# Graph attention in groups of four units instead of two

## The reference, cut to what matters

```python
for l in range(L):
    q = ((x @ Wq[l].T + bq[l]) * scaling).reshape(n, H, DH)
    k = (x @ Wk[l].T).reshape(n, H, DH)
    v = (x @ Wv[l].T).reshape(n, H, DH)
    scores = jnp.einsum('ehd,ehd->eh', q[tgt], k[srcidx])
    m = jax.ops.segment_max(scores, tgt, num_segments=n)
    p = jnp.exp(scores - m[tgt])
    s = jax.ops.segment_sum(p, tgt, num_segments=n)
    w = p / (s[tgt] + 1e-16)
    agg = jax.ops.segment_sum(w[:, :, None] * v[srcidx], tgt, num_segments=n)
    attn = agg.reshape(n, D) @ Wo[l].T + bo[l]
    ...
```

## Time and profile before

| | |
|---|---|
| median of 3 runs | 1277.33 us |
| all runs | 1277.33, 1277.38, 1270.37 us |
| the profiled execution | 1275.12 us |
| its span, first to last instruction | 1273.3 us |
| mean granted TensorE clock | 0.956 of 2.4 GHz |

### The profile page before, as it was taken

The page is one execution under the profiler, slowest core; times in us unless marked ns, Lnnn a source line. Parts: engine busy times, 40 slices in busy tenths (PEclk is TensorE's granted clock), DMA queues, the critical chain, the costliest instruction groups (busy, mean ns, idle before and its releaser), DMA issues.

```text
span 1273.3 us, 14957 instructions
## 1 busy us (share of the span) xinstructions
PE 1126.0 (88%) x5662; PEld 701.1 (55%) x5666; DVE 675.9 (53%) x1188; ACT 397.5 (31%) x538; POOL 201.2 (16%) x129
## 2 busy tenths in 40 slices
PE   2698999999988399999999999999989999999934
PEld 1122464447876388675566666643456666674412
DVE  7998521155556930542665556544145555663496
ACT  1001110216533211210554546411045454551103
POOL 5200000056950624200000000000000000003000
PEclk9799989989998799999999999999999999999967
DMA  5000101100020011001000001001100000100001
GB/s 190 17 0 1 34 1 33 33 0 34 1 67 0 1 33 67 34 1 66 1 1 1 1 1 68 1 21 46 33 1 1 1 1 1 34 1 19 1 0 66
DMA packets 16887, 28.98 MB, mean 23 GB/s; under 512 B 3834, under 2 KB 5050, under 8 KB 16570
## 3 DMA queue, kind: packets, MB, share of 16 engines
q1 hardware_dynamic: 14746, 26.03, 6.1%
q10 hardware_dynamic: 2080, 2.10, 0.5%
HBM read 26.02 MB, written 2.10 MB: 22 GB/s over the span
## 4 chain that ended last, share of the span: by engine, by line
PE 83%; DVE 11%; ACT 2%; issue 2%; DMA 1%; POOL 0%; DVEq 0%; SPq 0%; ACTq 0%
PE slots L1382 73%; PE slots L1449 10%; DVE PT L1209 1%; DVE KS L1199 1%; DVE st L857 1%; DVE XN L870 1%; DMA X<-in_x 1%; ACT KS L782 1%; DVE PT L921 0%; DVE SM L1263 0%; DVE X L1275 0%; DVE XT L1157 0%; DVE st L1280 0%; DVE XT L1178 0%; DVE st L847 0%
## 5 line engine op out<-in xcount | busy, mean ns | idle before, releaser
L1382 PE MATMUL slots<-XT,W 128*128 128x512 f32 x448 | 202.2, 605 | 0.0
L1382 PEld LDWEIGHTS slots<-XT,W 128*128 128x128 f32 x448 | 84.4, 193 | 105.5 <-issue 103.8
L1382 PE MATMUL slots<-PT 128*128 128x512 bf16 (+2 forms) x420 | 105.3, 381 | 31.0 <-issue 29.1
L876 DVE COPY PT<-slots 128x1024 f32<-128x1024 f32 x66 | 80.7, 1222 | 85.9 <-PE slots L1449 70.1
L1382 PE MATMUL slots<-KS,QS 64*128 64x512 f32 x768 | 108.4, 415 | 18.0 <-DVE KS L1199 9.9
L1382 PE MATMUL slots<-PT,XN 128*64 128x256 f32 x1024 | 117.6, 382 | 0.0
L601 POOL TENSOR_TENSOR QS<-QF,QS 128x512 fp32r<-128x512 f32 x16 | 20.6, 1286 | 555.1 <-PE slots L1449 359.9
L632 ACT ACTIVATE PT<-slots 128x1024 f32<-128x1024 f32 x70 | 71.6, 1023 | 106.8 <-PE slots L1449 54.3
L1382 PEld LDWEIGHTS slots<-KS,QS 64*128 64x128 f32 x768 | 73.3, 190 | 39.5 <-issue 10.0
L1382 PEld LDWEIGHTS slots<-PT,XN 128*64 128x64 f32 x1024 | 70.7, 137 | 42.9 <-issue 9.8
L1209 DVE CUSTOM_DVE_ANT_0 PT<-slots,MASK 128x1024 f32<-128x1024 f32 x64 | 75.8, 1222 | 31.7 <-PE slots L1382 31.7
(11 more groups left out here) (309 smaller groups left out, 1631.3 us busy)
## 6 DMA issues: line engine op xcount, KB each, us to landing
X<-in_x SPq DMA_DIRECT2D x1, 2048.0 KB, 8.4
W<-in_v SPq DMA_DIRECT2D x2, 1024.0 KB, 10.9
W<-in_k SPq DMA_DIRECT2D x2, 1024.0 KB, 10.1
W<-in_wout SPq DMA_DIRECT2D x2, 1024.0 KB, 5.2
W<-in_q SPq DMA_DIRECT2D x2, 1024.0 KB, 5.1
W<-in_gv SPq DMA_DIRECT2D x2, 1024.0 KB, 8.4
W<-in_gq SPq DMA_DIRECT2D x2, 1024.0 KB, 5.0
W<-in_gk SPq DMA_DIRECT2D x2, 1024.0 KB, 5.2
```

What stands on the lines that cost most here:

```text
L876: nc.vector.tensor_copy(dst, src).then_inc(dve_evacuated, 1)
L1382: return nc.tensor.matmul(o_, lhsT, rhs, start=start, stop=stop)
```

## The change

The list advances by four units at a time. Where it had two `turn`, two `score`, two `turn`, two `score`, it has four `turn` and then four `score`. The distance `LAG` = 4 between a unit's score and its transposition in the loop's counters stays. The other steps (`q`, `k`, `rsum`, `rsum_bc`, `agg`) go to the nearest places behind the four scores. No instruction is added or removed, and the code of the engines is the same.

```diff
 def attention_order():
 
     order = [("q", 0), ("q", 1), ("k", 0)]
-    for n in range(0, UNITS + LAG + 4, 2):
+    for n in range(0, UNITS + LAG + 8, 4):
         m = n - LAG
         if 0 <= m < UNITS:
-            order += [("turn", m), ("turn", m + 1)]
+            order += [("turn", m + i) for i in range(4)]
         if n < UNITS:
-            order += [("score", n), ("score", n + 1)]
-        if m >= 16 and m % 16 == 2:
+            order += [("score", n + i) for i in range(4)]
+        if m >= 16 and m % 16 == 4:
             order.append(("rsum_bc", m // 16 - 1))
-        if n % 8 == 2 and 8 <= n < UNITS - 8:
+        if n % 8 == 0 and 8 <= n < UNITS - 8:
             order.append(("q", n // 8 + 1))
-        if n % 16 == 6 and n < UNITS - 16:
+        if n % 16 == 4 and n < UNITS - 16:
             order.append(("k", n // 16 + 1))
         if m >= 16 and m % 16 == 0:
             order.append(("rsum", m // 16 - 1))
-        if m >= 4 and m % 4 == 0:
+        if 4 <= m <= UNITS:
             order.append(("agg", m // 4 - 1))
     return order
```

## The result

The changed kernel takes 1307.17 us (median of four, 1303.65 to 1309.12) against 1276.3 us before (1270.37 to 1277.38). The ratio is 1.0249, with a 95% interval from 1.0209 to 1.0288: slower, by 30.9 us between the medians. The profiled execution took 1307.08 us for a span of 1305.2, so the span grew by 31.9 us.

What follows compares the result with a forecast made beforehand. TensorE's own instruction stream and its standstills were taken to bound the kernel. Per layer 21.0 + 0.5 + 0.6 - 7.0 + 3.0 = +18.1 us, both +36.2, so 1277.3 + 36 = 1313 us, range 1298 to 1330.

Steps and rivals of the forecast that it cites:

- The stall: Before `turn` n + 3 in every group, TensorE waits 1.69 us for an exponential queued behind a copy on ScalarE.
- Merging: On TensorE, four transposed and four scored units take 6.67 against 6.96 us, 0.29 us less in each group.
- the forecast's rival: In the attention, no stall, so faster: -9.0 us a layer, 1259 us; 3% for faster by over 1%.
- Waits that go: TensorE's waits on keys, `nm` and `AG`, and at the layer's end, shrink or vanish: -7.0 us a layer.
- The wait of `project`: At the layer's end, `project` waits some 0.4 us for the copy of an `agg`, before 0.90 for unit 63's.
- Waits that come: Jobs behind four scores wait for slots on TensorE: +3 us a layer, ranging from 0 to 6.
- The first job behind four scores: It takes unit n's slot, freed at 3.04 against 2.96 us: 0.08 us each, 1.3 in all.
- The `rsum` without a `k`: Behind this 0.2 us job, the next waits 0.9 us for the slot of unit n + 1.
- the second pair waiting for its slot: Scores of n + 6 and n + 7 take unit n + 3's slot: 0 taken, 0.15 us a group kept for range.
- The total: Both layers add 36.2 us; the profiled execution would take 1311.3 us, the median 1313 us.
- The clock: Behind the stalls TensorE's clock falls to 1.2 GHz: 1353 us at all 32, 1333 at half; 6%.
- The 6%: Chance given to TensorE's clock falling behind the stalls, for 1353 us at all 32 or 1333 at half.

Runs made afterwards that it cites:

- Four experiments: Changed kernel with exponentials one place ahead: 1255.01 us; one place later: 1364.8 us; second unit's copy given to VectorE: 1255.65 us; three small copies before the fourth exponential: 1327.14 us.
- the first experiment: Changed kernel with ScalarE doing exponentials up to n, not n - 1, at `score` n: 1255.01 us, ratio 0.980; a repeat took 1258.17 us, ratio 0.985.
- the old rule: ScalarE does exponentials up to n - 1 at `score` n: changed kernel 1307.17 us; with the new one, up to n, 1255.01 us.
- the kernel with 1.79 us: Changed kernel with three small one-column copies put on ScalarE before the exponential of each group's fourth unit: 1327.14 us, ratio 1.037.

## Why the prediction was right

**The stall.** The forecast put the fourth unit's transposes at 4.40 us; they start at 4.35 (684.04 to 688.39). It put TensorE's free time at 2.71; with the exponential ahead four units take 3.65 where the forecast had 3.71. The idle time that the profile shows is 1.52 and not 1.69: 0.05 of it is this difference, and the rest comes from counting, since the profile counts from the modelled end of the last transpose (686.88) and the forecast from where the next could start (686.75). Four experiments move this one term, by removing it in two ways and enlarging it in two.

**Merging.** Four transposed and four scored units were to take 6.67 us against 6.96. They took 3.65 and 2.98. The layer without the stall is 821.74 - 606.97 = 214.8 us in the first experiment and 224.9 before: -10.1 us, where the forecast's rival had -9.0.

**Waits that go.** The three waits on the keys, the five on the mask pass and the one on `AG` went as listed; the 0.9 us on `nm` that are left are a new wait, the next term. The wait of `project` is 0.4 as worked out.

**Waits that come.** This is the term that was too large: +3 us a layer. The first job behind four scores was to lose 0.08 us and starts 2.97 to 3.00 us after them, 0.01 to 0.04 over the 2.96. The `rsum` without a `k` cost 0.86 of the 0.9, and the job behind each `rsum_bc` 0.2 us as forecast (693.53 - 692.38 = 1.15 against 0.93). One group of layer 0 has scores 0.24 us longer (3.28 and not 3.04), most likely the second pair waiting for its slot, though the profile names no wait. Together some 2 us. With 0.8 us less for the sixteen times 0.05 of the stall this makes the layer some +16.3 where +18.1 stood; it measured +16.6 and +16.5.

**The total.** Two layers give 33.1 and not 36.2 us. The 0.7 us by which each layer's first transposes came sooner stand in no term of the forecast. In layer 1 they are luck with the clock, and both together bring the sum near the +31.9 of the span. The forecast then put 2.2 us on top of the profiled execution, as the kernel before had its median above it; the changed kernel's median lies 0.1 us above its profiled execution. These small terms nearly all fell on one side, and make 1307 of 1313.

**The clock.** Held at 1.00 through all groups. The rows it was argued from showed waits of 1.66 and 2.44 us without a fall, but they were three waits, and the later experiments show that waits of 1.79 and 2.39 us can go either way. The 6% were fair, and the reason given for them was weaker than it read.

## What to carry to other kernels

When several engines walk one written list, a change of the list changes each engine's order, not only that of the engine for which it is meant. Before regrouping steps, follow every producer: which instruction now stands right before the one that somebody waits for, and what does that one wait for. An engine that is busy for 30% can hold up one that is busy for 90%, and the remedy may be a single index: here the regrouping cost 2.5% with the old rule and gained 1.5 to 2% with the new one.

## What the runs showed of the hardware

TensorE's granted clock can fall behind a wait of some 2 us, and the length of the wait alone doesn't decide it. With one idle time of 1.52 us in each group it stayed at 1.00 in both layers. With 1.79 us it fell to 1.2 GHz behind 8 of 30 waits, where the scores took 4.61 us and not 3.05. With 2.39 us its mean was 0.94 in layer 0's groups, with 10 of 16 waits followed by slow work, and 0.99 in layer 1's, with one of 16. Behind the wait of 2.53 us before layer 1's first scores the same kernel ran them in 4.61 us in one execution and in 3.02 in another. So a stall can have a second price, which isn't in proportion to its length and which one trace doesn't tell: 1.14 us more of it in 32 groups, 36 us by itself, cost 58 between the medians. Some of the spread has nothing to do with such stalls: the executions of the kernel with 1.79 us lie 15 us apart, and those of the kernel before, beside it, 10.
